# Layer-norm statistics merged into the key/value stage, queries double-buffered, value rounding moved beside them: one Trainium2 core

## The reference, cut to what matters

```
x = x + xattn(layernorm(x), ctx)
q = (x @ Wq + bq) / 4;  k, v = split(cond @ Wkv + bkv)
q = fq_sym(q, per head row);  k = fq_sym(k, per head row);  v = fq_sym(v, per column over all rows)
out = fq_unsigned(softmax(q @ k.T)) @ v;  out @ Wp + bp
fq_sym: s = max(|x|)/127;  round(x/s) * s
```

## Time and profile before

| what | us |
|---|---|
| median of 3 runs | 6581.19 |
| the profiled execution's own time | 6572.37 |
| its span, first to last instruction | 6570.9 |
| first GpSimd instruction of the query stage | 232.19 |
| first VectorE instruction of the value stage | 344.97 |
| first GpSimd instruction of the attention stage | 418.30 |
| VectorE busy over the span | 5686.5 (87%) |

### The profile page before, as it was taken

One profiled execution on the slowest core, in us unless ns is written; L12 is line 12 of the kernel. 1 busy time (PEld: TensorE's weight loads), 2 busy tenths in 40 slices (PEclk: granted clock), 3 DMA queues, 4 the chain that ended last, 5 costly groups with the idle time before them and its releaser, 6 DMA issues. The chain is left out here.

```text
span 6570.9 us, 141175 instructions
## 1 busy us (share of the span) xinstructions
PE 4523.2 (69%) x48970; PEld 2144.1 (33%) x49686; DVE 5686.5 (87%) x7938; ACT 4572.5 (70%) x4949; POOL 4505.6 (69%) x3196
## 2 busy tenths in 40 slices
PE   6736666666666666666666666666666645769999
PEld 3412222222222222222222222222222233454555
DVE  7579999999999999999999999999999955873222
ACT  3328888888888888888888888888888843331111
POOL 1238888888888888888888888888888833420000
PEclk9769999999999999999999999999999977989999
DMA  3137677677677677677777777766766740010000
GB/s 118 51 76 140 139 140 143 138 140 142 139 141 142 135 144 141 139 142 139 141 139 141 141 137 140 144 137 140 142 139 140 138 105 4 0 35 4 6 6 10
DMA packets 2231911, 735.21 MB, mean 112 GB/s; under 512 B 2175779, under 2 KB 2209412, under 8 KB 2225573
## 3 DMA queue, kind: packets, MB, share of 16 engines
q1 hardware_dynamic: 2196261, 576.08, 42.2%
q0 software_dynamic: 35456, 157.33, 13.2%
HBM read 168.97 MB, written 27.26 MB: 30 GB/s over the span
## 5 line engine op out<-in xcount | busy, mean ns | idle before, releaser
L803 DVE TENSOR_SCALAR_CACHE_REDUCE scores<-ring,step 128x2048 f32<-128x2048 f32 (+2 forms) x2560 | 4780.3, 1918 | 44.4 <-PE ring L730 28.0
L882 ACT ACTIVATE n_op<-scores,bias 128x2048 uint8<-128x2048 f32 x2048 | 4075.1, 1992 | 493.5 <-DVE m_rest L810 493.5
L678 POOL CAST nT<-pairs 128x2048 f16<-128x2048 uint8 x2048 | 3791.3, 1890 | 561.0 <-DMA pairs<-n_op 536.7
L730 PE MATMUL ring<-x_all,q_op 128*128 128x512 bf16 x7746 | 2153.7, 386 | 863.2 <-DVE scores L803 773.1
L730 PEld LDWEIGHTS ring<-x_all,q_op 128*128 128x128 bf16 x8192 | 683.0, 98 | 2021.1 <-DVE scores L803 1330.1
L727 PE MATMUL ring<-x_all,q_op 128*128 128x512 bf16 x1793 | 572.9, 390 | 808.0 <-DVE scores L803 780.3
L742 PE MATMUL pO<-nT,v_op 128*32 128x128 f16 x32768 | 660.1, 224 | 20.6 <-POOL nT L678 20.6
L742 PEld LDWEIGHTS pO<-nT,v_op 128*32 128x32 f16 x32768 | 478.5, 98 | 467.1 <-issue 359.2
L727 PEld LDWEIGHTS ring<-x_all,q_op 128*128 128x128 bf16 x2048 | 116.7, 97 | 1035.6 <-DVE scores L803 1028.3
L882 ACT ACTIVATION_READ_ACCUMULATOR n_op<-scores,bias 128x1 f32 x2048 | 384.7, 188 | 0.0
L1637 DVE TENSOR_TENSOR h_up<-h_gate,pUp 128x512 f32<-128x512 f32 x112 | 76.9, 687 | 298.2 <-ACT h_gate L1626 298.2
(11 more groups left out here) (194 smaller groups left out, 3293.2 us busy)
## 6 DMA issues: line engine op xcount, KB each, us to landing
x_all<-keys_transposed POOLq DMA_DIRECT2D x128, 768.0 KB, 8.4
v_st<-value_integers POOLq DMA_DIRECT2D x128, 256.0 KB, 3.5
pairs<-n_op SPq DMA_TRANSPOSE x2048, 2.8
keys_transposed<-kT_s POOLq DMA_DIRECT2D x32, 384.0 KB, 3.5
x_all<-in_x SPq DMA_DIRECT2D x2, 4096.0 KB, 14.9
cT<-in_ctx_T SPq DMA_DIRECT2D x32, 256.0 KB, 3.0
q_op<-queries_transposed POOLq DMA_DIRECT2D x384, 16.0 KB, 8.4
value_integers<-v_int SPq DMA_DIRECT2D x1, 4096.0 KB, 12.2
```

The costliest lines, as they stand in the source:

```text
L678: nc.gpsimd.tensor_copy(nT[par][:, j * EK:(j + 1) * EK, :].rearrange("p (a c) b -> p a c b", c=2), src).then_inc(s_un, 1)
L730: mm = nc.tensor.matmul(slot(t, j)[:, n * BANK:(n + 1) * BANK], q_op[b][:, t * P:(t + 1) * P], k_op[b][:, at + n * BANK:at + (n + 1) * BAN ...
L803: nc.vector.tensor_scalar(score[t % 2][:, at:at + width * BANK], slot(t, j)[:, 0:width * BANK], step[b][:, t:t + 1], None, ALU.mult, ALU.m ...
L882: nc.scalar.activation(n_op[par][:, j * EW:(j + 1) * EW], score[par][:, j * EW:(j + 1) * EW], ACT.Exp, bias=bias[par][:], scale=-1.0, accu ...
```

## The change

The loads of stage 1 are no longer waited for there; `x`, Wq and Wp are loaded in the key/value stage, and the statistics are taken there too. VectorE's quantisation keeps six operations. The bf16 casts go to ScalarE (`first_part`, `second_part`), the two subtractions to GpSimd (`first_remainder`, `second_remainder`). TensorE projects three steps ahead instead of two. The query stage gets two buffers of each kind and takes in the value stage; the clearing of the key operands becomes a stage of its own, a quarter on GpSimd and three quarters on VectorE.

```diff
 @block.sync, keys and values
                 load(0, 0)
                 load(1, 1)
+                sp.dma_start(x_all[:], x_t).then_inc(s_x, 16)
+                for dst, src in ((wq_sb, a["L0_xattn_Wq"]), (wp_sb, a["L0_xattn_Wp"])):
...
 @block.gpsimd
+                def first_remainder(it, i):
+                    pool.wait_ge(s_k0, after(it))
+                    pool.sem_inc(s_zero, 1)
+                    nc.gpsimd.tensor_tensor(heads(k_b[i][:]), heads(k_a[i][:]), part(i, 0), ALU.subtract).then_inc(s_kd, 1)
+                def second_remainder(it, i):
+                    pool.wait_ge(s_k1, after(it))
+                    pool.sem_inc(s_zero, 1)
+                    nc.gpsimd.tensor_tensor(part(i, 2), heads(k_b[i][:]), part(i, 1), ALU.subtract).then_inc(s_kp, 1)
...
+                first_remainder(0, 0)
+                first_remainder(1, 1)
+                second_remainder(0, 0)
+                with pool.Fori(0, NI // 2 - 1) as k:
                     for i in range(2):
                         it = k * 2 + i
+                        first_remainder(it + 2, i)
+                        second_remainder(it + 1, 1 - i)
+                        store(it, i)
...
 @block.tensor
                 project(0, 0, 0)
                 project(1, 0, 1)
-                with pe.Fori(0, NI // 2 - 1) as k:
+                project(2, 1, 0)
+                with pe.Fori(0, NI // 2 - 2) as k:
                     for i in range(2):
                         turn(k * 2 + i, i)
-                        project(k * 2 + i + 2, k + 1, i)
+                        project(k * 2 + i + 3, k + 1 + i, 1 - i)
...
 @block.scalar
                 def copies(it, i):
                     act.wait_ge(s_kv, after(it))
-                    act.wait_ge(s_kp, after(it - 2))
+                    act.wait_ge(s_kq, after(it - 2))
...
+                def first_part(it, i):
+                    act.wait_ge(s_kq, after(it))
+                    act.wait_ge(s_ktp, after(it - 2))
+                    nc.scalar.copy(part(i, 0), heads(k_a[i][:])).then_inc(s_k0, 1)
+                def second_part(it, i):
+                    act.wait_ge(s_kd, after(it))
+                    nc.scalar.copy(part(i, 1), heads(k_b[i][:])).then_inc(s_k1, 1)
...
+                with act.Fori(1, NI // 2 - 2) as k:
                     for i in range(2):
-                        evacuate(k * 2 + i, i, k)
-                        copies(k * 2 + i + 2, i)
+                        it = k * 2 + i
+                        copies(it + 3, 1 - i)
+                        second_part(it + 1, 1 - i)
+                        evacuate(it, i, k)
+                        first_part(it + 2, i)
...
 @block.vector
+                dve.wait_ge(s_x, 16)
...
+                dve.wait_ge(s_sd, 1)
+                nc.vector.reciprocal(rstd[:], std[:])
...
-                    dve.wait_ge(s_ktp, after(it - 2))
-                    link(nc.vector.tensor_copy(part[0], heads(k_a[:])))
-                    link(nc.vector.tensor_tensor(heads(k_b[:]), heads(k_a[:]), part[0], ALU.subtract))
-                    link(nc.vector.tensor_copy(part[1], heads(k_b[:])))
-                    nc.vector.tensor_tensor(part[2], heads(k_b[:]), part[1], ALU.subtract).then_inc(s_kp, 1)
...
 queries and values
+                for it in range(NI_Q):
+                    multiply(it)
+                    if it + 2 < NI_Q:
+                        project(it + 2)
+                    if it >= 1:
+                        turn(it - 1)
...
+                nc.vector.tensor_reduce(v_amax[:], v_f[:].rearrange("p t c -> p c t"), AX.X, ALU.max,
+                                        apply_absolute_value=True).then_inc(s_v, 1)
+                for it in range(NI_Q):
+                    queries(it)
+                    if it == V_FIRST + 1:
+                        value_steps()
+                    if V_FIRST + 3 <= it < V_FIRST + 3 + KT // VB:
+                        round_values(it - V_FIRST - 3)
...
+                    if it == NI_Q - 2:
+                        sp.wait_ge(s_vr, KT // VB)
+                        sp.dma_start(v_d.rearrange("h p n -> p h n"), v_int[:].rearrange("p h k d -> p h (k d)")
+                                     ).then_inc(s_vd, 16)
...
-                for i in range(2):
-                    nc.gpsimd.memset(k_op[i].bitcast(F32), 0.0)
+                nc.gpsimd.memset(k_area[:, 0:NK // 2].bitcast(F32), 0.0)
...
+                nc.vector.memset(k_area[:, NK // 2:2 * NK].bitcast(F32), 0.0)
```

More of the change, by code:

```diff
@@ L167, in build @@
         s_bp = sem("bias_parts", cs)
+        s_st = sem("statistics_query", cs)
+        s_sd = sem("deviation_query", cs)
         s_kv = sem("kv_ready", cs)
@@ L326, in build @@
         qs = ExitStack()
-        xn = sb("xn", [P, G, D], F32, qs)
-        xT = sb("xT", [P, G, DC, P], F32, qs)
-        q_f = sb("q_f", [P, G, D], F32, qs)
+        xn = [sb(f"xn{i}", [P, G, D], F32, qs) for i in range(2)]
+        xT = [sb(f"xT{i}", [P, G, DC, P], F32, qs) for i in range(2)]
+        q_f = [sb(f"q_f{i}", [P, G, D], F32, qs) for i in range(2)]
         q_amax = sb("q_amax", [P, G, H], F32, qs)
@@ L347, in build @@
         s_qts = sem("queries_transposed_copied", qs)
-        s_qst = sem("queries_stored", qs)
+        s_qst = [sem(f"queries_stored{i}", qs) for i in range(2)]
+        s_v = sem("value_steps", qs)
+        s_vp = sem("value_products", qs)
+        s_vi = sem("value_integers", qs)
+        s_vr = sem("values_rounded", qs)
+        VB = 8
+        V_FIRST = 2
         with nc.Block() as block:
@@ L410, in evacuate @@
-                def evacuate(it):
-                    act.wait_ge(s_qtp, it + 2)
-                    act.wait_ge(s_qst, 16 * it)
-                    nc.scalar.copy(qT_s[:].rearrange("p c g n -> p g c n"), pQT[:]).then_inc(s_qts, 1)
-                copies(0)
-                copies(1)
-                evacuate(0)
-                with act.Fori(2, NI_Q) as it:
-                    copies(it)
-                    evacuate(it - 1)
-                evacuate(NI_Q - 1)
+                    i = it % 2
@@ new lines, in evacuate @@
+                def evacuate(it):
+                    i = it % 2
+                    act.wait_ge(s_qtp, it + 1)
+                    if it >= 2:
+                        act.wait_ge(s_qst[i], 16 * (it // 2))
+                    nc.scalar.copy(qT_s[i][:].rearrange("p c g n -> p g c n"), pQT[i][:]).then_inc(s_qts, 1)
+                copies(0)
+                for it in range(NI_Q):
+                    if it + 1 < NI_Q:
+                        copies(it + 1)
+                    scaled(it)
+                    if it >= 2:
+                        evacuate(it - 2)
@@ L422, in _ @@
+                for it in range(NI_Q - 2, NI_Q):
+                    evacuate(it)
             @block.vector
             def _(dve):
-                dve.sem_inc(s_qi, 1)
-                with dve.Fori(0, NI_Q) as it:
-                    LINKS = 5
-                    done = [0]
-                    def link(ins):
-                        done[0] += 1
-                        ins.then_inc(s_qch, 1)
-                        dve.wait_ge(s_qch, it * LINKS + done[0])
-                    dve.wait_ge(s_qc, it + 2)
-                    link(nc.vector.tensor_reduce(q_amax[:], heads(q_f[:]), AX.X, ALU.max, apply_absolute_value=True))
+                done = [0]
@@ L435, in _, with link, queries @@
+                def link(ins):
+                    done[0] += 1
+                    ins.then_inc(s_qch, 1)
+                    dve.wait_ge(s_qch, done[0])
+                def queries(it):
+                    i = it % 2
+                    dve.wait_ge(s_qc, it + 1)
+                    link(nc.vector.tensor_reduce(q_amax[:], heads(q_f[i][:]), AX.X, ALU.max, apply_absolute_value=True))
                     link(nc.vector.tensor_scalar(q_st[:], q_amax[:], 1.0 / 127.0, EPS_STEP, ALU.mult, ALU.max))
```

293 lines of the change are left out of this document (164 added, 129 removed).

## The result

The changed kernel takes 6750.9 us (median of 4 runs, 6745.01 to 6754.1), against 6575.93 for the kernel before in the same comparison: a ratio of 1.0268, with a 95% interval of 1.0249 to 1.0286. It is slower by 2.7%. The profiled execution took 6754.1 us, its span 6752.6.

A forecast was written before the change was run, and what follows sets the result against it. VectorE, busy 87% mostly in the unchanged attention, was taken as the bound, so only the attention's start mattered: +224.4 (loop, start included) - 58 + 5.7 = +172 on 6572.4, giving 6744.5 us; range 6655 to 6835.

The forecast's parts named there:

- The closed round: Key/value loop: TensorE, ScalarE and GpSimd work lies end to end from turn to turn, 11.0 us a step against 5.59.
- the walk: Key/value loop: following the three in-order lists of TensorE, ScalarE and GpSimd together from one turn to the next.
- the rival that had the least chance in the prediction: Key/value loop: evacuation and first part not in the round, step about 7.7 us, 6572 us in all; chance 0.02.
- Its length: Key/value loop step at full clock: turn to key copy 4.75, ScalarE 3.85, GpSimd 2.4, sum 11.0 us.
- The clock: Key/value loop: TensorE's bursts begin at the low clock, adding 2.65 us, so a step takes 13.65 us.
- the clock full throughout: Rival for the key/value loop: 11.0 us a step, turn(29) 77 us earlier, 6668 us in all; chance 0.10.
- The start: Before the key/value loop: first key quantised at 33.1 instead of 43.92, 10.8 us gained, statistics starting at 19.2.
- Turn 0: Key/value loop: TensorE's turn for step 0, forecast at 44.4 us.
- Queries and values: Merged query and value stage: 128 us from its start to the attention instead of 186.1, so -58 us.
- The clearing: Clearing of key operands, now standing alone: VectorE's memset 5.3 us plus 0.4, so +5.7 us.
- The 0.4: Clearing stage: 0.4 us allowed for the block's change, beside VectorE's memset.
- the handovers and last turns: Key/value loop: 0.3 us a step for three hand-overs; last two turns 6.2 and 1.2 us, without projection before them.

The follow-up runs named there:

- The experiments on the order alone: Changed kernel with GpSimd's second_remainder ahead of first_remainder, 6612.16 us; with ScalarE's copies last in the step, 6542.32 us; with both, 6518.9 us.
- The first of them: Changed kernel with one swap in GpSimd's list, second_remainder(it+1) ahead of first_remainder(it+2): 6612.16 us, ratio 1.0045 to the kernel before.
- the filler: Changed kernel with its orders, TensorE doing 26 more unused 128x512 bf16 products after each projection: 6680.04 us, ratio 1.0145 to the kernel before.
- the kernel with both orders: Changed kernel with second_remainder ahead of first_remainder on GpSimd and copies(it+3) last on ScalarE: 6518.9 us, ratio 0.9886 to the kernel before.

## Why the prediction was right

The forecast was 6745 us for the likeliest case; 6750.9 was measured. As a difference it was +172 us, and the medians lie 175.0 apart. Point by point:

- *The closed round* held, edge by edge: the step above shows the order that the walk gave. The experiments on the order alone are its proof, since they run the same instructions. The first of them is also the rival that had the least chance in the prediction, a step of about 7.7 us "as if GpSimd took the second remainder first": so ordered, the steps at the high clock take 7.8 us. What that rival left out is that the clock falls in others even then, so that the kernel took 6612 and not 6572 us.
- *Its length.* Turn to key copy at the high clock 4.75; ScalarE 222.69 - 218.86 = 3.83 where 3.85 was forecast. A cast takes 0.63, the evacuation's rate and not the key copy's, but the next operation begins 0.52 after it (219.82 to 220.34), so that little of this is left in the sum. GpSimd 225.26 - 222.69 = 2.57 where 2.4 was forecast: its subtraction with a bf16 operand takes 1.142, not the 1.042 of the all-f32 row. An estimate from the figure in section 3.1 of the Trainium skill's page "GPSIMD Engine Reference" is 1.12, nearer than the row. The 0.17 us of GpSimd make 5 us in all.
- *The clock.* 2.65 us a step was forecast; turn to key copy is now 218.86 - 211.56 = 7.30, 2.55 more than 4.75, and the filler took 2.42 away. The bursts-between-waits pattern that the page "TensorE: Matmul & The Clock Gate" of the Trainium skill describes in its section "HAM oscillation" is what this trace shows, with a granted clock of 0.74 in the mean. With the clock full throughout the time would have been about 6680, as the filler kernel's: inside the range but not the forecast. It was luck in part that the step came out at 13.67 us against 13.65: GpSimd was put 0.17 too low and the clock 0.10 too high.
- *The start* was the term that was missed most: 10.8 us were forecast and 8.4 came, since the statistics begin at 21.86 and not at 19.2. SyncE's list has Wkv and two context tiles ahead of x now, where x came first; it took 17.6 us from issue (4.24) to landing, and 14.3 before. Turn 0 came 2.7 us later than forecast for it, and that carried through.
- *Queries and values*: 130.1 us against 128. VectorE sets the pace in the middle as forecast (from 505 to 560 it waits for 2.5 us in all), and the last steps are TensorE's at the low clock: its product for pair 15 held VectorE for 5 us.

```profile
575.86 0.69 DVE L546 TENSOR_REDUCE q_amax<-q_f 128x32 f32<-128x512 f32 x1 [5.02 <-ACT q_f L516]
```

- *The clearing*: VectorE's memset 5.18 us against 5.3, the stage 6.8 against 5.7, because 1.6 us stand beside the memset here and not 0.4: it begins 1.35 us after GpSimd's share, and the attention 0.26 after its end. The 0.4 had no row behind it.

The errors sum to 7.4 us at the start of the attention (597.68 against 418.30 + 172 = 590.3), of which the start is 2.7, the handovers and last turns 1.5, the query stage 2.1 and the clearing 1.1. All four go the same way, so nothing cancels there. Over the whole program the two profiled executions differ by 181.7 us, 9.7 more than forecast, of which the other 2.3 stand behind the start of the attention, in code that is the same.

## What to carry to other kernels

When work is split over several in-order engines, write down each list and follow one item from a wait back to itself: the sum along the longest closed round, divided by the steps it spans, is the step, however idle each engine looks. Put into each list first what the next item of the critical engine needs, and last what waits for the farthest producer: here two changes of order were worth 3.4% (6750.9 to 6518.9 us) with no instruction changed. A round that left TensorE waiting cost twice here, since the next burst started at the low clock (2.42 us of 13.67). And look again after each step: once the round was gone, the engines that now worked at the same time slowed each other.

## What I had not expected of the hardware

- One GpSimd memset of 6.92 us held a VectorE tensor_scalar of 0.43 us for 6.52 us; in pieces of 1024 elements it held none longer than 0.91 us in the lines shown. In the loop, VectorE's f32 rounding beside a GpSimd subtraction took 1.26 us instead of 0.43 in the kernel with both orders, each of 25 times from 60 to 190 us, while the reduction kept its 0.69.
- Waits of only 3.1 us between bursts already brought the clock down in some of the steps (0.89 on average), so that steps with the same instructions took 7.8 or 9.5 us.
- Useless products made the kernel 71 us faster, as they kept the clock up.
